# Two-layer decoder kernel: a query mask moved from the matrix engine to VectorE, steps of a batch in other slots, and drains left out

## The reference

```
scores = jnp.einsum('bhqc,bhkc->bhqk', q, k) / math.sqrt(K_CHANNELS)
scores = jnp.where(attn_mask == 0, jnp.float32(-10000.0), scores)
p_attn = jax.nn.softmax(scores, axis=-1)
```

## Time and profile before

| | us |
|---|---|
| median of 3 runs | 1647.9 (1640.52 to 1651.41) |
| the profiled execution, its own time | 1650.96 |
| its span, first to last instruction | 1649.2 |
| mean granted clock of TensorE | 0.923 |

### The profile page before, as it was taken

One profiled execution on the slowest core, in us unless ns is written; L12 is line 12 of the kernel. 1 busy time (PEld: TensorE's weight loads), 2 busy tenths in 40 slices (PEclk: granted clock), 3 DMA queues, 4 the chain that ended last, 5 costly groups with the idle time before them and its releaser, 6 DMA issues. The chain is left out here.

```text
span 1649.2 us, 29414 instructions
## 1 busy us (share of the span) xinstructions
PE 1379.6 (84%) x9381; PEld 906.9 (55%) x9491; DVE 979.9 (59%) x2625; ACT 620.6 (38%) x1413; POOL 441.0 (27%) x612
## 2 busy tenths in 40 slices
PE   2468999999999963899999964688888877699997
PEld 1245666666665531555556633455555643488886
DVE  5367777787776615222222224568878753478886
ACT  0124445545544430223222323346555543334331
POOL 2243342342341101111111013555555420101100
PEclk9689999999999975999999986789999987699999
DMA  3233443443432107521111114755444420300000
GB/s 89 61 67 64 67 73 58 69 74 58 71 69 38 24 12 246 185 77 36 33 33 33 29 40 90 167 115 117 105 109 113 102 57 17 82 1 14 9 5 26
DMA packets 165943, 112.76 MB, mean 68 GB/s; under 512 B 32786, under 2 KB 155922, under 8 KB 165664
## 3 DMA queue, kind: packets, MB, share of 16 engines
q1 hardware_dynamic: 150880, 99.04, 26.9%
q0 software_dynamic: 3408, 9.31, 2.3%
q10 hardware_dynamic: 11504, 2.53, 0.9%
HBM read 46.48 MB, written 12.45 MB: 36 GB/s over the span
## 5 line engine op out<-in xcount | busy, mean ns | idle before, releaser
L893 ACT ACTIVATE first_probs<-pair 128x512 f32<-128x512 f32 x320 | 189.3, 598 | 221.8 <-PE pair L409 212.0
L450 DVE TENSOR_REDUCE first_negmax_x<-bank 128x2 f32<-128x512 f32 x256 | 172.6, 681 | 51.9 <-PE bank L394 50.6
L394 PE MATMUL bank<-kept_stack_cross 96*128 96x256 bf16 x768 | 153.3, 282 | 11.2 <-DVE second_negmax_a L448 2.8
L1920 ACT ACTIVATE second_probs<-pair 128x512 f32<-128x512 f32 x192 | 113.9, 598 | 125.6 <-PE pair L409 103.0
L409 PE MATMUL pair<-kept_stack_cross 98*128 98x256 bf16 x768 | 150.6, 279 | 3.1 <-DMA kept_stack_cross<-second_rows_x 1.1
L1442 PE MATMUL pair<-kept_w,experts_hidden_t 128*128 x312 | 141.1, 595 | 0.0
L450 DVE TENSOR_REDUCE second_negmax_x<-bank 128x2 f32<-128x512 f32 x128 | 88.5, 692 | 57.4 <-PE bank L394 49.6
L394 PEld LDWEIGHTS bank<-kept_stack_cross 96*128 96x128 bf16 x768 | 74.7, 102 | 74.5 <-issue 23.6
L1483 ACT ACTIVATE experts_hidden_t<-bank,kept_b 128x128 f32<-128x128 f32 x156 | 44.4, 367 | 187.4 <-PE bank L1417 187.4
L1397 POOL DMA_INDIRECT experts_expert_rows<-x_mid,kept_row_of x39 | 37.1, 951 | 276.4 <-PE bank L1409 250.1
L1442 PEld LDWEIGHTS pair<-kept_w,experts_hidden_t 128*128 128x128 f32 x312 | 59.9, 192 | 75.6 <-issue 75.6
(11 more groups left out here) (449 smaller groups left out, 3081.7 us busy)
## 6 DMA issues: line engine op xcount, KB each, us to landing
kept_stack_self<-first_parts_a SPq DMA_DIRECT2D x128, 64.0 KB
kept_w<-in_L_ffn_W SPq DMA_DIRECT2D x16, 512.0 KB, 9.1
kept_w<-in_L_ffn_W SPq DMA_DIRECT2D x8, 1024.0 KB, 9.5
kept_stack_self<-second_parts_a SPq DMA_DIRECT2D x128, 64.0 KB
kept_stack_cross<-first_parts_x_k SPq DMA_DIRECT2D x96, 64.0 KB
kept_stack_cross<-first_parts_x_q SPq DMA_DIRECT2D x96, 64.0 KB
kept_stack_cross<-second_parts_x_k SPq DMA_DIRECT2D x96, 64.0 KB
kept_stack_cross<-second_parts_x_q SPq DMA_DIRECT2D x96, 64.0 KB
```

What stands on the lines that cost most here:

```text
L394: mm = pe.matmul(out, q, k, start=mask is None, stop=True, skip_group_check=True)
L450: return dve.tensor_reduce(negmax[:, 2 * n:2 * n + 2], bank[:, :].rearrange("p (m t) -> p m t", t=D), AX.X, ALU.max, negate=True)
L893: act.activation(probs[i % RING][:, :], key_bank[i % 2][:, :], ACT.Exp, scale=att.scale).then_inc(probs_made, 1)
L1920: act.activation(probs[i % RING][:, :], key_bank[i % 2][:, :], ACT.Exp, scale=att.scale).then_inc(probs_made, 1)
```

## The change

In the first layer the query scores of a cross head are written without the mask matmul. VectorE's `cross_maximum` adds the mask itself: for each half of a bank one `tensor_tensor_reduce` adds 256 mask values (bf16, SBUF) to 256 scores (f32, PSUM), multiplies by -1, writes the result in bf16 to one of 16 new tiles `masked` (never read), and takes the minimum, which is the negative maximum. The mask matmul of the second pass stays. Thirty-five steps of a batch get other slots in the first layer and thirty in the second. In the second layer the drain at the end of VectorE's slot is left out, and `negmax_x` has two buffers by turns.

```diff
+        masked = [sb(f"masked_{a}", [P, D], BF16) for a in range(16)]
...
-        COPY_CROSS_OUT, CROSS_RECIPS, LAY_RECIPS, SPREAD_SUMS, CROSS_HEADS, MAKE_Y, CROSS_SUM, ROOT_X, CROSS_END = 89, 92, 93, 96, 97, 99, 100, 101, 105
+        COPY_CROSS_OUT, CROSS_RECIPS, LAY_RECIPS, SPREAD_SUMS, CROSS_HEADS, MAKE_Y, CROSS_SUM, ROOT_X, CROSS_END = 88, 92, 93, 97, 97, 100, 100, 102, 106
...
-                query_scores(pe, CROSS0, score_bank[i % 2], t["stack_cross0"][b % 3], n, ident16[:, :], mask_q).then_inc(scored, 1)
+                query_scores(pe, CROSS0, score_bank[i % 2], t["stack_cross0"][b % 3], n, ident16[:, :], None).then_inc(scored, 1)
...
-                reduce_maxima(dve, CROSS0, negmax_x[:, :], score_bank[i % 2], n).then_inc(reduced, 1)
+                for a in range(2):
+                    ins = dve.tensor_tensor_reduce(masked[(2 * i + a) % 16][:, :], score_bank[i % 2][:, a * D:(a + 1) * D], t["mask_q"][:, a, :], -1.0, 3.0e38,
+                                                   ALU.add, ALU.min, negmax_x[:, 2 * n + a:2 * n + a + 1])
+                ins.then_inc(reduced, 1)
...
-        negmax_x, two_x = sb("negmax_x", [P, 2 * YG]), sb("two_x", [P, P], BF16)
+        negmax_x, two_x = [sb(f"negmax_x_{u}", [P, 2 * YG]) for u in range(2)], sb("two_x", [P, P], BF16)
...
-        CROSS_VALUES, CROSS_VALUES_END, COPY_CROSS_OUT, CROSS_RECIPS, LAY_RECIPS, SPREAD_SUMS, CROSS_HEADS, MAKE_Y, CROSS_SUM, CROSS_MOMENTS, ROOT_X, CROSS_END = 56, 58, 59, 61, 62, 64, 65, 66, 67, 68, 68, 70
+        CROSS_VALUES, CROSS_VALUES_END, COPY_CROSS_OUT, CROSS_RECIPS, LAY_RECIPS, SPREAD_SUMS, CROSS_HEADS, MAKE_Y, CROSS_SUM, CROSS_MOMENTS, ROOT_X, CROSS_END = 56, 59, 59, 61, 62, 65, 65, 67, 67, 67, 69, 69
...
                 if (b := slots.batch_at(s, LATENT_END)) is not None:
                     latent_end(b)
-                dve.drain()
```

More of the change, by code:

```diff
@@ new lines, in first_layer_attentions @@
+        TURN_HEADS, COPY_HEADS, MAKE_O, OWN_SUM, ROOT_A, OWN_END = 26, 26, 28, 28, 29, 29
+        LOAD_CONTEXT, MAKE_CROSS_K, ROTATE_K, SPLIT_KEYS, STACK_KEYS = 6, 14, 16, 17, 23
+        MAKE_CROSS_Q, ROTATE_Q, SPLIT_QUERIES, STACK_QUERIES = 31, 31, 33, 38
+        MAKE_CROSS_V, COPY_CROSS_V, CROSS_TWO, TURN_CROSS_MAXIMA, CROSS_ROWS = 59, 59, 59, 61, 61
+        CROSS_VALUES = (73, 82, 86, 88)
+        COPY_CROSS_OUT, CROSS_RECIPS, LAY_RECIPS, SPREAD_SUMS, CROSS_HEADS, MAKE_Y, CROSS_SUM, ROOT_X, CROSS_END = 88, 92, 93, 97, 97, 100, 100, 102, 106
@@ L601, in first_layer_attentions @@
+        STORE_ROWS, TURN_X2, COPY_X2, MAKE_LOGITS, KEEP_LOGITS = 107, 108, 108, 110, 113
         query_lane = slots.lane(OWN_SCORES, CROSS_SCORES, SELF0.banks, CROSS0.banks)
@@ L656, in _ @@
             ident, ident16 = t["ident"], t["ident16"]
-            mask_q, mask_t = (t[n][:, :, :].rearrange("p a k -> p (a k)") for n in ("mask_q", "mask_t"))
+            mask_t = t["mask_t"][:, :, :].rearrange("p a k -> p (a k)")
             def turn_rows(b, s):
@@ L1637, in second_layer_attentions @@
+        STORE_ROWS, TURN_X5, COPY_X5, MAKE_QUERIES, COPY_QUERIES, STORE_QUERIES = 69, 71, 71, 73, 73, 73
+        LOAD_CHUNK, CHUNK_HIGH, CHUNK_LOW = 0, 8, 14
         query_lane = slots.lane(OWN_SCORES, CROSS_SCORES, SELF1.banks, CROSS1.banks)
```

30 lines of the change are left out of this document (11 added, 19 removed).

## The result

The changed kernel takes 1569.5 us (median of four runs, 1563.2 to 1572.3) against 1649.7 us for the kernel before in the same session: a ratio of 0.951, 95% interval 0.945 to 0.957. That is 80 us less. The forecast was 1619 us and its range ended at 1594; the sign was right, the size was not, and the time lies outside the range.

The account below looks back on a forecast made before the run. PE was taken to bound the first layer, VectorE the second, with VectorE becoming the first layer's bound after the edit. 1650.96 - 10 (first layer) - 22 (second layer) = 1619 us, range 1594 to 1662.

Parts of the forecast that it names:

- The bank's price on VectorE: First layer's cross maxima: a bank costs VectorE 0.88 us instead of 0.61, adding 4.3 us per batch.
- PE's need: First layer: without 16 mask matmuls of 0.22 us, PE's need falls from at most 30.83 to 27.3 us per batch.
- VectorE's need plus 0.3: First layer's pace: VectorE's 30.3 us per batch plus 0.3 for remaining waits, 30.6 against 30.83, -2.5 us over 11 batches.
- The drains: Second layer, ends of VectorE's slots: a drain costs 0.16 us where work waits; leaving them out gives -19.5 us.
- rival (c): Second layer: removing drains brings nothing, as VectorE waits for PE or the next instruction is held anyway; 1638 us, chance 0.09.
- The moves of the second layer: Second layer's slot changes: some pairs further apart, others closer; allowed -0.2 us per batch, -2.5 us.
- Build-up and run-down: First layer's ends: -6.5 us for three run-down batches, -1 for build-up; second layer's drain gain counted for 13 of 16 batches.
- (a): First layer: a bank costs VectorE more than taken, above about 1.15 us; 1682 us at the 1.24 upper bound; chance 0.12.
- (b): First layer: a bank costs VectorE 1.0 to 1.15 us, giving 1640 to 1664 us; chance 0.16.
- (d): Both layers' edits at their cheap ends: 0.82 us per bank, second layer -38 us; 1593 us, chance 0.10.
- (e): Second layer: SP's second cross stack comes 1 to 2 us late each batch, giving back 22 us; 1641 us, chance 0.07.
- (f): PE's clock drops with less work; at 0.98 PE needs 27.9 us, still below VectorE, so nothing follows; no chance given.

Follow-up runs that it names:

- The two halves: Kernel before with only the second layer's slot moves ahead of slot 0 (1647.0 us), or only those from the context's load on plus self-attention's own row (1652.5 us).

## Why the prediction was right or wrong

**The bank's price on VectorE** is the first of the two terms that failed. I wrote 0.88 us with 0.82 as lower bound; it is 0.68. The error is mostly in the reads: I gave each 0.07 us, from a one-column instruction (whose row reads 0.08, so by my own rows the price should have been 0.90 and the bound 0.84). They run beside the pass behind them and add nothing. The pass itself is 0.34, where I took 0.37. Near my price the chip gives 1597 us (the run with a drain behind each bank, 0.91), at its own 1570. That is 26 us for 0.23 us a bank, so by proportion, an estimate, some 23 for the 0.20 by which I was off, of the 50 us by which I missed. The bound was no bound, because nothing in the trace of before excluded zero for the read. With the price as low as that the path changes too: VectorE would need 26.0 + 16 x 0.07 = 27.1 us a batch, less than PE's 27.3, so VectorE does not become the bound of the first layer. By my own sum that is 27.6 us a batch and -43 us for the layer, where its whole edit measured -45.

**The rest of the first layer's sum** held in the main. PE's need fell to about 27 us as worked out; VectorE's waits fell from 53.6 to some 17 us, not under 10; the wait for the sums' transfer went, as argued from its four slots. "VectorE's need plus 0.3" was 0.9 us too high with the bank at 0.91 (31.1 against 30.2). I missed that the slots matter more than as cover: without them, the mask edit gives 1 us, not 10.

**The drains.** The overlap of 0.08 us and the price of 0.16 were right (0.18 measured). The product 94 x 0.16 x 1.3 = 19.5 us was not: 0 us with the old slots, 13 with the new. I had subtracted the waits that were there, but not asked where VectorE's saved time would be spent. It went into waits for PE, 33.5 us instead of 16. That was rival (c) in its first form, to which I gave 0.09, and for the drains alone it is what happened. In its second form, the Trainium skill's "VectorE: DVE Perf Modes", section "The DRAIN you can't avoid", has the next operation start only when the pipe is empty, and the pair above at 0.25 us behind a duration of 0.33 does not bear that out here; the same section lets an operation that isn't held start earlier, which is what these rows show and what my sentence on it had left out.

**The moves of the second layer** are the second failed term, as large as the first: -2.5 us allowed, -26 measured with the drains kept. I judged them pair by pair, "several further apart, others closer", and let them nearly cancel. My reading now, which no run tests pair by pair, is that a pair that is late costs its wait in every batch and a pair with room gives nothing back, so that they cannot be summed with signs. The two halves show that it is not enough to mend some of them: each alone gives nothing. What the whole table does by itself is shown: VectorE's waits fall from 20.4 us in 210 to about 4 in 200, and the steps from batch to batch, 19.4 to 24.8 us in the first eight before, are 18.0 to 21.1 in the first eleven. Which pairs are needed together stays open.

**Build-up and run-down.** I gave the second layer's last batches nothing, as VectorE is idle there for most of the time. The first and the last split of the cross maxima of the second layer in the kernel before (timeline of VectorE):

```profile
1072.25 0.17 DVE L457 CAST second_two_x<-second_negmax_x 128x16 bf16<-128x16 f32 x1
...
1380.41 0.17 DVE L457 CAST second_two_x<-second_negmax_x 128x16 bf16<-128x16 f32 x1
```

That is 308.2 us, and 1297.35 - 1028.99 = 268.4 after: 40 us less. The last three steps took 1380.41 - 1326.61 = 53.8 us and take 44.5, so 9 of the 40 lie there. Neither engine is full in these (PE 71.23 and VectorE 39.81 of 100 us), so I take it that handovers set their time; no run tests that apart. In the first layer the last three steps gave 8 us (78.8 to 534.38 - 463.86 = 70.5), where I had 6.5.

**The rivals.** (a) and (b) fell with the price. (d), both edits at their cheap ends, 1593 us, was nearest, and still 23 us short. The bound of (b) has a slip: 1.15 us a bank gives 1619 + 47.5 = 1666.5, not 1664. (e) did not come about: from 1047 to 1236 us PE has no wait for a cross stack, and 1.8 us for the self-attention's. (f) did not either.

## What to carry to other kernels

Before an edit that frees one engine is priced, look for transfers and handovers that are laid out in slots: the freed time can be given back whole at the first one that does not fit. Do not take a transfer's time for fixed either: the same one took 4.0 us to be ready before, and 5.2 with the mask edit. Change the work and the slots together and measure them together. Here the work alone gave 1 us, the slots alone 14 and both 45, so a part that brought nothing by itself has not been shown useless. And an operation that no row shows has no lower bound but zero: a price that decides which engine is the bound is worth one run of its own.

## What the runs showed of the hardware

- The read of VectorE's accumulator (0.08 us) costs nothing in the sequence: the next pass starts at the same moment as the read (301.21 and 301.21), in a row of passes that all carry an accumulator.
- An add of a bf16 mask from SBUF to f32 scores from PSUM with a minimum over 256 columns takes 0.34 us from start to start, so two of them take 0.68 where one plain reduction over 512 columns takes 0.61: the mask costs VectorE 0.07 us a bank.
- A drain costs 0.18 us behind a 64-column instruction, and 0.23 behind a masked pass (0.91 - 0.68).
